# Batch loads, identity matrices and one stack's clearing moved inside the start of an attention and feed-forward kernel

## Time and profile before

| | |
|---|---|
| median of 3 runs | 163.2 us (162.35 to 163.65) |
| the profiled execution | 163.05 us, of which the span from first to last instruction is 161.2 us |
| PE busy | 143.8 us (89% of the span) |
| DVE busy | 136.7 us (85%) |
| ACT busy | 125.4 us (78%) |
| POOL busy | 104.0 us (65%) |
| chain that ended last, by engine | PE 55%, DVE 12%, ACT 11%, POOL 8%, issue 7%, DMA 4% |
| TensorE clock granted | 1.00 in all 40 slices |

### The profile page before, as it was taken

How to read it: one execution, slowest core, us unless ns; L and a number is a source line. 1 busy time by engine, 2 the same in 40 slices (tenths; PEclk the granted TensorE clock), 3 DMA queues, 4 the chain that set the end, 5 groups by cost and what they waited for, 6 DMA issues and landing times.

```text
span 161.2 us, 4126 instructions
## 1 busy us (share of the span) xinstructions
PE 143.8 (89%) x1402; PEld 66.7 (41%) x1402; DVE 136.7 (85%) x204; ACT 125.4 (78%) x255; POOL 104.0 (65%) x185
## 2 busy tenths in 40 slices
PE   6968998998999999999997999979889966999893
PEld 2644553433333333433333333332323342665672
DVE  6788998898999989789997999993398788999972
ACT  3042377899899899989889889886999966998970
POOL 5889625848818818806898997822313579689920
PEclk9999999999999999999999999999999999999999
DMA  3994896457255345533233000000000000001012
GB/s 107 278 206 97 262 294 191 141 141 213 71 135 147 85 108 173 192 76 82 62 74 86 3 3 4 5 5 4 3 0 4 0 0 2 0 33 39 33 65 98
DMA packets 19904, 14.19 MB, mean 88 GB/s; under 512 B 2360, under 2 KB 18800, under 8 KB 19884
## 3 DMA queue, kind: packets, MB, share of 16 engines
q1 hardware_dynamic: 16940, 11.52, 25.7%
q10 hardware_dynamic: 2624, 2.17, 5.2%
q0 software_dynamic: 320, 0.25, 1.0%
HBM read 6.17 MB, written 1.07 MB: 45 GB/s over the span
## 4 chain that ended last, share of the span: by engine, by line
PE 55%; DVE 12%; ACT 11%; POOL 8%; issue 7%; DMA 4%; SPq 1%; ACTq 0%; DVEq 0%; POOLq 0%
PE y_ps L1073 14%; PE s_ps L1034 13%; ACT probs L570 5%; PE t_ps L1053 5%; DVE maxes L944 4%; PE s_ps L1164 4%; PE t_ps L1006 3%; DMA bias_scr<-bias_parts 2%; PE t_ps L1094 2%; ACT hid_sq L675 2%; PE y_ps L1114 2%; PE t_ps L1183 2%; PE t_ps L1015 2%; DVE hid L878 2%; PE t_ps L1203 2%
## 5 line engine op out<-in xcount | busy, mean ns | idle before, releaser
L944 DVE TENSOR_REDUCE maxes<-s_ps 128x4 f32<-128x1024 f32 x64 | 76.0, 1218 | 6.8 <-PE s_ps L1034 6.6
L570 ACT ACTIVATE probs<-t_ps 128x512 f32<-128x512 f32 x118 | 65.9, 591 | 8.6 <-PE t_ps L1053 6.2
L1034 PE MATMUL s_ps<-k_st,q_st 64*128 64x256 bf16 x256 | 44.7, 274 | 1.0 <-DMA k_st<-bias_scr 0.5
L1053 PE MATMUL t_ps<-q_st,k_st 64*128 64x256 bf16 x236 | 42.5, 274 | 3.3 <-ACT probs L570 1.6
L1073 PE MATMUL y_ps<-probs,v_pad 128*18 128x256 f32 x512 | 38.6, 384 | 0.2 <-ACT probs L570 0.2
L1034 PEld LDWEIGHTS s_ps<-k_st,q_st 64*128 64x128 bf16 x256 | 15.8, 94 | 29.6 <-issue 16.0
L1164 PE MATMUL s_ps<-w_q,ffn_x 128*128 128x512 bf16 x64 | 17.2, 380 | 2.9 <-DVE hid L878 2.4
L523 POOL TENSOR_TENSOR hw<-hid,ln_bc 128x512 f32<-128x512 f32 x8 | 10.2, 1273 | 12.0 <-DVE hid L867 8.9
L1053 PEld LDWEIGHTS t_ps<-q_st,k_st 64*128 64x128 bf16 x236 | 14.0, 94 | 8.3 <-ACT probs L570 3.6
L438 POOL TENSOR_SCALAR nm_parts<-maxes 128x16 bf16<-128x16 f32 x16 | 3.3, 207 | 21.6 <-DVE maxes L944 21.5
L1073 PEld LDWEIGHTS y_ps<-probs,v_pad 128*18 128x18 f32 x512 | 9.6, 96 | 14.2 <-issue 11.6
(11 more groups left out here) (116 smaller groups left out, 245.6 us busy)
## 6 DMA issues: line engine op xcount, KB each, us to landing
q_st<-parts SPq DMA_DIRECT2D x48, 64.0 KB, 2.7
k_st<-parts SPq DMA_DIRECT2D x33, 64.0 KB, 2.4
w_f<-in_wgT ACTq DMA_DIRECT2D x2, 512.0 KB, 4.7
w_f<-in_wuT SPq DMA_DIRECT2D x2, 512.0 KB, 4.3
w_f<-in_wdT SPq DMA_DIRECT2D x2, 512.0 KB, 4.9
out<-o_sb SPq DMA_DIRECT2D x8, 128.0 KB, 1.7
k_st<-parts ACTq DMA_DIRECT2D x15, 64.0 KB, 3.1
x_sb<-in_x SPq DMA_DIRECT2D x2, 256.0 KB, 3.9
```

Of the source, the lines that this page charges most:

```text
L570: act.activation(probs[:, t % NP_RING].rearrange("p e t -> p (e t)"), src, ACT.Exp, scale=SCALE)\
L944: dve.tensor_reduce(dst[:, :, s, :], s_ps[:, c % 2], AX.X, ALU.max).then_inc(s_maxed, 1)
L1034: mm = pe.matmul(s_ps[:, c % 2, i, e, :], q_st[b % RING][rows, hp, qt * P:qt * P + P], k_st[b % RING][rows, hp, :], start=True, stop=True)
L1053: mm = pe.matmul(t_bank(bank["t", t])[:, e * T:e * T + T], k_st[b % RING][rows, hp, kt * P:kt * P + P], q_st[b % RING][rows, hp, :], start ...
```

## The change

The last group of x is loaded after the bias rows of the first stack. The two identity matrices are finished by POOL before it waits for the mask. DVE clears the stacks 1 and 2, and POOL the stack 3, after its first `negate_maxes`; the loads into stack 3 wait for a semaphore of their own. Four of the matmuls on zeros in front of the first scores are gone.

```diff
+        last_zeroed = sem("last_zeroed")
 ...
         def load_high(queue, b, side):
             if b >= RING:
                 queue.wait_ge(unit_ready, unit["t", 16 * (b - RING + 1) - 1] + 1)
+            elif b == RING - 1:
+                queue.wait_ge(last_zeroed, 2)
             elif b:
                 queue.wait_ge(q_zeroed, b + 1)
                 queue.wait_ge(k_zeroed, b + 1)
 ...
             load_x(2)
-            load_x(3)
             load_high(sp, 0, 0)
             sp.wait_ge(bias_step, 7)
             sp.dma_start(bias_scr, bias_parts[:, :, :, :].to_broadcast([B, 2, 3, T])).then_inc(bias_stored, 16)
             load_low(sp, 0, (0,))
             load_bias(0)
+            load_x(3)
             load_rows(1)
 ...
+            pool.wait_ge(ident_ready, 2)
+            for m in (ident_b, ident_f):
+                pool.affine_select(out=m[:, :], in_=m[:, :], compare_op=ALU.not_equal, fill=1.0,
+                                   base=0, pattern=[[-1, P]], channel_multiplier=1).then_inc(ident_ready, 1)
+
             pool.wait_ge(mask_in, 32)
 ...
-            pool.wait_ge(ident_ready, 2)
-            for m in (ident_b, ident_f):
-                pool.affine_select(out=m[:, :], in_=m[:, :], compare_op=ALU.not_equal, fill=1.0,
-                                   base=0, pattern=[[-1, P]], channel_multiplier=1).then_inc(ident_ready, 1)
             pool.memset(ones_f[:, :], 1.0).then_inc(small_const, 1)
 ...
             def load_constant_rows(b):
                 if b < RING:
-                    pool.wait_ge(q_zeroed, b + 1)
-                    pool.wait_ge(k_zeroed, b + 1)
+                    pool.wait_ge(last_zeroed, 2)
 ...
                 if n >= 0 and has(n + 3):
                     load_constant_rows(n + 3)
+                if n == -1:
+                    pool.memset(q_st[RING - 1][:, :, :].rearrange("p h t -> p (h t)").bitcast(f32), 0.0).then_inc(last_zeroed, 1)
+                    pool.memset(k_st[RING - 1][:, :, :].rearrange("p h t -> p (h t)").bitcast(f32), BF16_ONES)\
+                        .then_inc(last_zeroed, 1)
 ...
-            for r in range(1, RING):
+            for r in range(1, RING - 1):
                 clear_stacks(r)
 ...
             project_qk(3)
-            keep_array_busy(4)
```

## The result

Over 20 runs of each, the changed kernel took **163.56 us** (median; 163.02 to 165.02) and the kernel before 163.21 (162.33 to 165.53). The ratio is 1.0047, with a 95% interval of 1.0024 to 1.007: a little slower, within 1%, and the other way than forecast. The predicted 162.4 was 1.2 us too low, and 163.5, the end of the range, just missed it. The profiled execution took 163.52 us, its span 161.7.

The account below looks back on a forecast made before the run. The start's bias write and read-back were taken to bound the kernel; first scores 0.99 us earlier, of which 0.72 survives ACT's copy of v(3). 163.05 - 0.72 = 162.33, or 162.5 from the median: 162.4 us, range 161.5 to 163.5.

Parts of the forecast that it names:

- What bounds the kernel: At the start: bias write to DRAM, 3.90 us, then bias rows read back, 2.24 us, hold the first scores until 14.91.
- Rival C: Bias write slow of itself, or late x holds `project_qk(5)` at 18.7 or beyond; 0 to 0.3 us left, 163.1; 20%.
- No large idle time in which an earlier start could get lost: After the first scores: PE busy 10.00 of 10.00 us from 15 to 25, so moving the scores moves the end.
- Two clearings fewer on DVE: Before the first reduction: DVE free 2.14 us earlier, at 13.3; the start needs all three edits together.
- Nothing after that goes by a clock of its own: After the first scores: all later waits are for work fed by the same chain.
- losses that I can't name: Anywhere in the kernel: unspecified losses, given 6%.
- `project_qk(5)` held by ACT's copy of v(3): After the first scores: the bank is free at 18.22, so `project_qk(5)` starts at 18.27, 0.72 us earlier, not 0.99.
- Rival B: ACT's issues speed up, v(3) is placed 0.5 us earlier, the full 1.2 of the start arrives: 162.0; 15%.
- Bias write with x out of the way: In SP's queue: the write takes 2.9 us instead of 3.90, landing at 11.53; first scores 0.99 us earlier, at 13.92.
- Identities and fillings on POOL, the late x group: Identities hidden before the mask, fillings (2.1 us) in POOL's idle time, x landing between 16.2 and 18.7: no cost.
- Rival D: Before the first scores: PE idles 1.40 us, its clock drops for some 4 us, costing 2 us: 165.1; 4%.
- Worth nothing by itself: Before the first scores: removing the four matmuls on zeros gives 0.46 of the 0.99 us, and nothing alone.

Follow-up runs that it names:

- e2: The kernel before with only the clearing of stack 3 moved from DVE to POOL: 163.3 us, ratio 1.0032.
- e12: The kernel before without its four matmuls on zeros, nothing else changed: 163.62 us, ratio 1.0007.
- e1: The changed kernel with two unread one-column memsets on DVE, its list as long as before; three runs: 162.36, 163.41 and 162.97 us.
- e9: As e1 but with four memsets on DVE instead of two: 163.35 us in one execution.
- b2: The kernel before, unchanged, run again for a third trace: 163.74 us.
- e3: The kernel before with x's last group behind the bias rows and no matmuls on zeros, DVE still clearing all stacks: 163.4 us, ratio 1.0011.
- e6: The changed kernel with an unread 512-column memset on POOL before its rounding near 134 us: 163.91 us, ratio 1.0042.
- e10: e1 with the four matmuls on zeros put back before the first scores: 162.77 us, ratio 0.9994.
- e11: e1 with three matmuls on zeros where PE waits for the first rows of maxima: 163.43 us, ratio 1.0015.

## Why the prediction was wrong, step by step

- **What bounds the kernel: a mis-sized term.** The forecast took 3.90 + 2.24 us as the price of now, which was one execution's. In the other two traces of before the write was back by 11.4, PE had no gap, and the first scores stood behind the zeros at 14.3. Against those, ACT's v(3) leaves 0.16 us of the 0.72. An estimate of the mean, from the five traces of the kernel before or of it with one edit of e2 or e12 (shifts near 23 us of 0, -0.60, -0.63, e2 -0.47 and e12 +0.13, mean -0.31) and the -0.77 of the changed kernel: 0.46 us gained. In executions with an early write it is near nothing, as the lowest times say: 162.14 to 162.32 for e1, 162.15 to 162.40 for the kernel before. Rival C had the size for these, 0 to 0.3 left, for another reason: the write was slow in some executions only.
- **"No large idle time in which an earlier start could get lost": failed twice.** The view of stretches gave PE 10.00 us busy of 10.00. But 1.20 us of these were four matmuls on zeros (L1114) at 15.79 and 23.16, work that nobody waits for, so the row hid that much slack: a busy share has to be read without them. And the rows of maxima landed 1.9 us after their issue there, and 2.60 in the changed kernel's trace, 3.20 in e9, 3.90 in b2. What the start gains can be lost at these landings, and they scatter by more than the whole gain. Such a landing moved b2 by 1.4 us, e3 by 1.0 and e9 by 1.0.
- **Two clearings fewer on DVE: the room was sized right, its worth and its price were wrong.** DVE was free at 13.24, 2.14 us earlier, as worked out. But "Were they kept, DVE would hold the maxima at 15.38 and the start would gain nothing" holds for the first reduction only: e3 keeps the clearings and is 0.67 ahead near 23 us. So the start did not need all three edits together, and this one brought some 0.10 us. **The step that failed** is the sentence behind the stretches: "Nothing after that goes by a clock of its own; all later waits are for work that the same chain feeds." It put the price of this edit behind the start at nothing. What the runs showed in its place: with DVE's list two shorter, its sequencer pauses for 0.30 us at 134 us with no semaphore behind it, POOL's rounding gets its turn first, and `hw` takes 0.61 us longer. e2 has this loss by itself, e1 is without it. No rival had it; it falls under the 6% for "losses that I can't name", and its 0.92 us turned the sign. The sum with it: 0.92 less 0.46 is +0.46, and +0.35 was measured between the medians; for executions with an early write 0.92 less 0.16 is +0.76, and between the lowest it is 163.02 - 162.33 = +0.69. Nor is e1 against the changed kernel at odds: the mean of its three ratios is 0.9993, which is 0.0054 or 0.9 us below 1.0047.
- **`project_qk(5)` held by ACT's copy of v(3): right.** 18.27 forecast, 18.23 measured, with the wait named. Rival B (ACT moves too) fell: v(3) was placed at 17.78, 0.05 earlier.
- **Bias write with x out of the way: right within its bounds.** 2.9 forecast, at most 2.74 measured.
- **Identities and fillings on POOL, the late x group: right.** Hidden, with 0.63 and 2.42 us to spare; no wait for x. It landed at 15.6, before the forecast's 16.2 to 18.7; the 6.4 us in that sum was a transfer of 256 KB, not one of its size of 384.
- **Rival D, the clock: its mechanism is real, its place was not.** The gap before the first scores didn't lower the granted clock in the profiled execution. The one spell in a trace came at 28 us, in e6. The zeros themselves held the first scores by 0.64 us (14.26 in e10, 13.62 in e1), but near 23 us only 0.06 of it is left (-0.66 against -0.72). "Worth nothing by itself" holds for the matmuls on zeros in the medians (e12, 1.0007) and isn't settled for the number of spells.

Open: what the pause is (a fetch of instructions would explain a place fixed by their count, but only the place was shown, that one or four memsets also clear it, and that an instruction load moves with it); what makes the rows of maxima land 1.9 to 3.9 us after their issue; what decides the tie, since e10 and e11 meet as e1 does; and what sets off a spell of the lower clock. No version was measurably faster than before: the best, e1, had 0.9972, 1.0014 and 0.9993. The version that these readings point to, the change with DVE's clearings kept and the zeros left in, was not run.

## What to carry to other kernels

Before a transfer at the head of the chain is priced, take the trace of the same kernel two or three times: a landing of 3.9 us in one can be 2.7 in the next, and that difference was most of the forecast here. When a stretch looks full, take matmuls on zeros out of it before saying that there is no slack. When two instructions are taken out of an engine's list, look far behind the edit, at pairs of engines that start heavy SBUF work within 0.05 us of each other: here a delay of 0.3 us decided who goes first, and cost more than the edit brought. Pad the list to its old length as an experiment: it tells whether an unexplained loss comes from the work or from the list.

## What the runs showed of the hardware

- A pause that costs 0.30 us in DVE's sequencer with no semaphore behind it, 120 us after the edit, in the traces of all four kernels whose DVE list was two instructions shorter, and in none of fourteen others. A load of 8 KB on an instruction queue starts 1.03 to 1.06 us after `h_os` in the four, and within -0.10 to +0.23 us of it in the others.
- DVE's product of two SBUF tiles, 128x512 f32, takes 0.69 us when it has its turn first and 1.30 to 1.61 when POOL's rounding of 128x1024 has; the rounding takes 1.12 us first and 1.57 to 1.64 second. With POOL starting 0.36 us ahead, POOL was first (three traces); with 0.04 to 0.05 us, DVE was first in twelve traces and POOL in two.
- POOL's select on 128x128 took 0.28 us early, and 0.52 and 0.76 in the place it had before, when DVE was at work on the split of batch 0.
- The bias write took 2.7 us or less up to 4.2 (e12, 8.50 to 12.71) with the same transfers in front of it, and loads of rows of maxima took 1.9 to 3.9.
- The granted clock at 0.52 for 3.4 us cost 1.5 us (e6, 28.0 to 31.4). PE's last wait of over 0.3 us before it was one of 0.77 us, 2.2 us earlier; a wait of 1.00 us at the same place in the changed kernel's trace was followed by no such spell.
